# One column's shift moved from POOL to ScalarE in a gated cross-attention and expert kernel

## The reference, cut to what matters

```
ln    = layernorm(x)                                   # per row
xij   = sigmoid(si[:, :, None] + sj[:, None, :] + b)    # si, sj = ctx @ Wi, ctx @ Wj
x     = x + tanh(g_xattn) * (0.6 * xij + 0.4 * ln)
gate, e = max and argmax of softmax(layernorm(x) @ wg)  # 8 experts, one per row
x     = x + tanh(g_ffn) * gate * (layernorm(x) @ W[e].T + b[e])
```

## Time and profile before

| | us |
|---|---|
| median of 3 runs | 616.62 |
| lowest and highest of them | 616.19, 617.62 |
| the profiled execution, its own time | 614.38 |
| span of the profiled execution | 612.7 |
| PE busy in the span | 512.1 |
| DVE busy | 404.0 |
| POOL busy | 361.6 |
| ACT busy | 293.0 |

### The profile page before, as it was taken

One profiled execution on the slowest core, in us unless ns is written; L12 is line 12 of the kernel. 1 busy time (PEld: TensorE's weight loads), 2 busy tenths in 40 slices (PEclk: granted clock), 3 DMA queues, 4 the chain that ended last, 5 costly groups with the idle time before them and its releaser, 6 DMA issues.

```text
span 612.7 us, 14916 instructions
## 1 busy us (share of the span) xinstructions
PE 512.1 (84%) x2889; PEld 418.8 (68%) x2890; DVE 404.0 (66%) x529; ACT 293.0 (48%) x426; POOL 361.6 (59%) x537
## 2 busy tenths in 40 slices
PE   5576677685404999999999999999999999999990
PEld 4465566564303888887888888788888888888870
DVE  0867557765786777777777577777657757764230
ACT  2586464654313445544554454555445544453330
POOL 3686888789621465555555655556556465555652
PEclk9599678868755999999999999999999999999995
DMA  7942777592789588898878698787759877875530
GB/s 247 387 169 97 263 254 253 209 296 111 269 295 231 151 253 217 246 257 239 240 239 238 188 232 245 236 258 238 228 153 268 221 220 205 242 231 166 162 126 8
DMA packets 87751, 134.63 MB, mean 220 GB/s; under 512 B 11696, under 2 KB 69552, under 8 KB 87728
## 3 DMA queue, kind: packets, MB, share of 16 engines
q1 hardware_dynamic: 71504, 80.28, 47.0%
q0 software_dynamic: 15264, 54.06, 24.9%
q10 hardware_dynamic: 960, 0.00, 0.1%
HBM read 100.49 MB, written 35.91 MB: 223 GB/s over the span
## 4 chain that ended last, share of the span: by engine, by line
PE 41%; DVE 14%; issue 13%; POOL 11%; ACT 9%; ACTq 5%; DMA 3%; POOLq 1%; DVEq 1%; SPq 0%
PE pair L1153 34%; DVE xt L877 3%; DVE pair L885 3%; ACT rb L700 3%; ACT xt L692 3%; POOL table L485 2%; PE pair L1076 2%; DVE raw L798 2%; DMA gates<-in_L_xattn_b 2%; POOL scal L520 2%; DVE xr L809 2%; POOL scal L523 2%; PE pair L1067 1%; ACTq L733 1%; POOL xr L477 1%
## 5 line engine op out<-in xcount | busy, mean ns | idle before, releaser
L1153 PE MATMUL pair<-wt,xt 128*128 x1728 | 403.0, 397 | 28.5 <-DVE xt L877 26.0
L1153 PEld LDWEIGHTS pair<-wt,xt 128*128 128x128 f32 x1728 | 327.4, 190 | 103.8 <-issue 29.9
L531 POOL TENSOR_TENSOR rows<-rows,rb 128x1024 f32<-128x1024 f32 x37 | 89.4, 2416 | 3.0 <-ACT rb L714 1.6
L877 DVE TENSOR_TENSOR xt<-pair,xt 128x1024 f32 (+1 forms) x38 | 46.5, 1224 | 62.2 <-ACT xt L692 62.2
L686 ACT ACTIVATE wt<-pair 128x1024 f32 x56 | 57.5, 1028 | 55.9 <-DVE pair L885 51.7
L714 ACT ACTIVATE rb<-bias_bc,scal 128x1024 f32 (+1 forms) x37 | 46.0, 1244 | 71.2 <-POOL scal L527 71.2
L892 DVE TENSOR_TENSOR wt<-pair,wt 128x1024 f32 x56 | 67.9, 1212 | 13.0 <-ACT wt L686 13.0
L1076 PE MATMUL pair<-ident,xr 128*128 128x128 f32 x256 | 44.1, 328 | 32.2 <-DVE xr L809 32.2
L885 DVE STREAM_TRANSPOSE pair<-w_raw 128x1024 f32<-128x1024 f32 x56 | 69.4, 1239 | 1.0
L1076 PEld LDWEIGHTS pair<-ident,xr 128*128 128x128 f32 x256 | 36.4, 173 | 39.1 <-DVE xr L809 31.2
L295 POOL DMA_DIRECT2D rows<-table x38 | 23.2, 610 | 56.8 <-issue 28.4
(11 more groups left out here) (138 smaller groups left out, 408.5 us busy)
## 6 DMA issues: line engine op xcount, KB each, us to landing
w_raw<-in_L_ffn_W SPq DMA_DIRECT2D x264, 128.0 KB, 3.2
xb<-table SPq DMA_DIRECT2D x156, 128.0 KB
rows<-table POOLq DMA_DIRECT2D x38, 520.0 KB, 5.2
xr<-in_x SPq DMA_DIRECT2D x32, 512.0 KB, 6.3
ctx_in<-in_ctx SPq DMA_DIRECT2D x8, 512.0 KB, 6.9
bias_bc<-in_L_ffn_b SPq DMA_DIRECT2D x8, 512.0 KB, 6.2
out_x<-rows,scatter_row POOLq DMA_INDIRECT x36, 3.7
table<-xr,pos POOLq DMA_INDIRECT x32, 5.5
```

The lines of the kernel that those rows point to most:

```text
L531: nc.gpsimd.tensor_tensor(rows[:, k, 0:H], rows[:, k, 0:H], rb[:, :], ALU.add).then_inc(base_ready, 1)
L877: nc.vector.tensor_tensor(xt[:, at, 1, :, :].rearrange("p a k n -> p (a k n)"), ps[:, :], xt[:, at, 0, :, :].rearrange("p a k n -> p (a k ...
L1153: last = nc.tensor.matmul(out_ps[r % 2][:, HALF * h:HALF * (h + 1)], xt[:, r % RING, x_part, k, :], wt[:, bass.ds(par, 1), w_part, k, HALF ...
```

## The change

The shift `ln_b` is made on ACT by one ACTIVATE of one column (Identity with a scale column and a bias column), and the linear part on POOL subtracts it. On ACT the shift of tile t+2 stands in round t behind half_tanh(t+3) and the logits copy, and ahead of copy_turned(t). It waits for its tile's tanh and for the group's scaled mean; norm_scalars ends in a semaphore (`scales_of_tile`) where it ended in a wait of POOL on itself. The linear part waits for `shift_ready` where it waited for `th_ready`. One small DVE instruction at the start goes (`nc2h`), and the constant `c2h` takes its place. The statistics stay six tiles ahead, norm_scalars stays on POOL.

```diff
-                link(nc.gpsimd.tensor_tensor(ln_ma[:, four], of_group(g, MEAN), ln_a[:, four], ALU.mult))
+                nc.gpsimd.tensor_tensor(ln_ma[:, four], of_group(g, MEAN), ln_a[:, four],
+                                        ALU.mult).then_inc(scales_of_tile, 1)
 
             def linear(t):
                 s = slot_of(t)
-                pool.wait_ge(th_ready, t + 1)
-                link(nc.gpsimd.tensor_scalar(ln_b[:, t:t + 1], xr[:, s, TH:TH + 1], nc2h[:, 0:1], ln_ma[:, t:t + 1],
-                                             ALU.mult, ALU.subtract))
+                pool.wait_ge(shift_ready, t + 1)
                 nc.gpsimd.tensor_scalar(xr[:, s, 0:H], xr[:, s, 0:H], ln_a[:, t:t + 1], ln_b[:, t:t + 1],
-                                        ALU.mult, ALU.add).then_inc(lin_ready, 1)
+                                        ALU.mult, ALU.subtract).then_inc(lin_ready, 1)
...
+            def shift(t):
+                act.wait_ge(th_ready, t + 1)
+                act.wait_ge(scales_of_tile, t // GR + 1)
+                nc.scalar.activation(ln_b[:, t:t + 1], xr[:, slot_of(t), TH:TH + 1], ACT.Identity,
+                                     scale=c2h[:, 0:1], bias=ln_ma[:, t:t + 1]).then_inc(shift_ready, 1)
+
...
+            act.wait_ge(scales_ready, 1)
             for t in range(RTH - 1):
                 half_tanh(t)
+                if t:
+                    shift(t - 1)
             for t in range(T):
                 g, r = t // GR, t % GR
                 if t + RTH - 1 < T:
                     half_tanh(t + RTH - 1)
                 if r == 1 and g > 0:
                     logits_copy(g - 1)
+                if t + RTH - 2 < T:
+                    shift(t + RTH - 2)
                 copy_turned(t)
...
-            nc.vector.tensor_scalar(c2h[:, :], th2[:, 0:1], MIX / 2 / H, None, ALU.mult)
-            nc.vector.tensor_scalar(nc2h[:, :], th2[:, 0:1], -MIX / 2 / H, None, ALU.mult).then_inc(scales_ready, 1)
+            nc.vector.tensor_scalar(c2h[:, :], th2[:, 0:1], MIX / 2 / H, None, ALU.mult).then_inc(scales_ready, 1)
```

More of the change, by code:

```diff
@@ L83, in build @@
         c2h = sb("c2h", [P, 1])
-        nc2h = sb("nc2h", [P, 1])
         minus_half = sb("minus_half", [P, GR])
@@ L214, in build @@
         lin_ready = sem("lin_ready")
+        scales_of_tile = sem("scales_of_tile")
+        shift_ready = sem("shift_ready")
         xc_ready = sem("xc_ready")
```

## The result

The changed kernel takes 683.03 us (median of 3 runs, 683.01 to 683.92) against 616.62; the ratio is 1.110 with an interval of 1.107 to 1.114. The prediction of 616.8 us, 0.2 us slower with a range of 614.2 to 618.9, was 66 us too low.

A forecast was written before the change was run, and what follows sets the result against it. ACT's queue was taken to set the early end of the first stage and POOL the late end; +1.4 early, nothing in the middle and −1.2 late gave +0.2 on 616.62, so 616.8 us, range 614.2 to 618.9.

The forecast's parts named there:

- the late gain wins: Rival: ACT hides its shifts early (0.2), POOL's late relief reaches DVE's limit (2.36); 614.6 us, chance 0.26.
- ACT stands still: Rival: a group's first shift blocks ACT until POOL's scaled means are done; 618.6 us, chance 0.16.
- not relieved: Rival: POOL's earlier 1024-column steps only meet DVE's additions sooner, late gain zero; 618.0 us, chance 0.10.
- One shift on ACT: One-column ACTIVATE on ACT: 0.39 us from start to semaphore, 0.29 us of ACT's queue (bounds zero and 0.39).
- Early, +1.4: ACT's queue up to the logits copy at 46.29: shifts and waiting add 1.4 us, bounds 0.2 and 2.7.
- Late, −1.2: POOL, 109 to 156 us: 11 shifts go, 2.1 us later start at tile 21; end 1.2 us sooner.
- the bounds 0.4 to 2.36: Late gain: 0.4 us is what holds at tile 28; 2.36 is DVE's waits for POOL, the most obtainable.
- The step of 2.23 us: POOL's linear part of tile 28 before the change: 2.23 us instead of 1.20, read as stretched by DVE's tanh addition.
- The statistics, six tiles ahead,: Middle, 48 to 107 us: this lead covers later stores and loads, cost nothing; without it DVE loses up to 2.1 us.

## Why the prediction was wrong

**The failed step: the linear part was never priced.** The part-by-part sum took L477 at "the usual 1.20" after the change. The diff gives it another second operation, and POOL has no (multiply, subtract) wider than one column in the trace of before. That was an operation that the trace doesn't show, and it got neither bounds nor a sentence. Measured: 3.79 us, 32 × 2.6 = 83 us of POOL's time, 79 us at the end when changed alone. Each rival ("the late gain wins", "ACT stands still", "not relieved") took the old price too, so none could come near. (The first one's sum also has a slip that changes nothing: with the 0.2 us that its sentence gives for the early end it is 614.5, not 614.6.)

**What bounds the kernel.** The reading that the first stage's gain or loss goes unchanged to the end held to 2 us: the last tanh is added 67.6 us later (223.30 against 155.75), the end comes 69.6 later.

**One shift on ACT.** 0.39 us and 0.29 of queue forecast, 0.38 and 0.28 to 0.29 measured. The handover, counted as 0.49 for ACT's part and both ends, was 0.59 us of POOL's idle time, in the changed kernel and in the one whose step adds; 0.1 too low.

**Early, +1.4.** The mechanism was there, and the size in one execution of three: the logits copy comes 1.42 us later with all shifts on ACT (48.09 against 46.67), and 2.38 and 2.80 later in the other two kernels with early shifts (49.05, 49.47), where ACT waited 1.11 us for PE at a granted clock of 0.83. The linear part of tile 3 is at 32.32 (forecast 32.0). The prediction took PE's clock as given and has no term for it. At the end the early shifts cost 2.9 us with the added step, where 1.4 and the 0.5 seen with the added step make 1.9; the interval, from 1.8 on, does not exclude that. That the later shifts bring the lower clock about is only seen, not tested.

**Late, −1.2.** Turned round in the kernel with late shifts alone: +2.4 (0.9 to 3.3 by the interval). The 2.1 us that POOL was to start late at tile 21 were there: from the start of its tanh to that of its linear part it is 1.80 us before (107.72 to 109.52) and 3.93 with all shifts on ACT and a step that adds (110.92 to 114.85). The linear part was stretched less and not more: its mean over the first stage is 1348 ns (1380 before), over the late stage (112 to 159 us) 1297, where more than 1461 had been expected.

The overlap that "the change doesn't relieve POOL" spoke of hit DVE instead: 1.7 us on one addition that is on the path. Without it the late shifts gain 0.8 us from tile 23 to 31, and nothing that the medians can tell from no change (−0.4 us, interval −1.8 to +0.6). The direction of the overlap was the step that failed here: the bounds 0.4 to 2.36 excluded a loss with no reason but that POOL had less to do. The step of 2.23 us that the prediction read as one that starts in an addition began 0.05 us ahead of it; steps that do start in one are mostly stretched, and in the three cases where POOL's was not, DVE's addition was. In the profiled execution the rest of the loss goes with PE's clock behind tile 31, which is not traced to the change. With all shifts on ACT the late loss does not show (29.57 us against 29.63), so how the 5.3 us of that kernel divide stays open.

**The statistics, six tiles ahead,** cost nothing that the trace after shows: no wait of DVE's statistics for a load is among its longest groups of waits from 20 to 235 us.

## What to carry to other kernels

Price an instruction by its engine, shape, type *and* its operations: when a sign moves from one operand into the operation, find a row with that very operation at that width, or give it bounds as wide as an unknown instruction has. On POOL keep a scale and a shift as multiply and add (here 1.20 against 3.8 us), and put the sign into the one-column operand. When an engine is relieved, ask what it will now run beside: the gap that its old step left was DVE's, and filling it cost 1.7 us on one addition, more than the 0.4 of the step that went. And read more than one execution before a microsecond is put down to a change: two kernels that are alike up to tile 31 were 2.3 us apart at tile 7, at a granted clock of 1.00 and of 0.67.

## What the runs showed of the hardware that was not expected

- POOL's TENSOR_SCALAR over 128x1024 f32: multiply, add in either order 1.20 us; multiply, subtract 3.81; subtract, multiply 3.81; multiply, max 3.79; with constants 1.05 and 3.64. One operation alone, a multiplication or a subtraction, takes 2.85, longer than multiply and add together.
- At one column the pairs are hardly told apart: 386 ns in the median for multiply, subtract, 349 for multiply, add.
- When a wide POOL step (multiply, add) and a tanh addition of DVE overlap, mostly the later of the two pays: POOL in 51 cases in which it started from 0.05 us ahead of the addition to 0.93 us into it (1.37 to 2.30 us for 1.20), DVE in 14 in which POOL started 0.22 to 0.64 us ahead (1.62 to 2.04 for 1.23). Three times DVE paid, with 2.98 or 2.99, though POOL's step started 0.70 to 0.72 us into its addition: each time a store's descriptors were being made on POOL when the addition began, and the step followed on them.
- TensorE at its lower clock needs 1.97 us for the turn of a tile that takes 1.09 at the full one, and in two pairs of executions the stage's last tile then took 1.30 us longer.
